# Input weights in 4 KB runs, identity and vectors on ScalarE's queue, and x1's shift as an addition

## The reference

```python
u = layernorm(x) @ W_in.T + b_in
s_t = tanh(u_t + s_(t-1) * gamma + beta)        # 1024 steps, one after another
x1 = x + layernorm(states @ W_out.T + b_out)
gate = silu((layernorm(x1) @ q(gate_w)) * gate_scale)
up = (layernorm(x1) @ q(up_w)) * up_scale
out = x1 + layernorm(((gate * up) @ q(down_w)) * down_scale)
```

## Time and profile before

| | |
|---|---|
| Median of 3 runs | 557.77 us (557.42 to 558.75) |
| The profiled execution | 557.68 us |
| its span | 555.9 us |
| PE busy | 537.8 us, 97% |
| DVE busy | 446.1 us, 80% |
| ACT busy | 374.8 us, 67% |
| POOL busy | 247.6 us, 45% |
| DMA | 39.92 MB in 25333 packets |

### The profile page before, as it was taken

The page is one execution under the profiler, slowest core; times in us unless marked ns, Lnnn a source line. Parts: engine busy times, 40 slices in busy tenths (PEclk is TensorE's granted clock), DMA queues, the critical chain, the costliest instruction groups (busy, mean ns, idle before and its releaser), DMA issues.

```text
span 555.9 us, 11947 instructions
## 1 busy us (share of the span) xinstructions
PE 537.8 (97%) x2958; PEld 456.6 (82%) x2958; DVE 446.1 (80%) x2608; ACT 374.8 (67%) x2317; POOL 247.6 (45%) x372
## 2 busy tenths in 40 slices
PE   7999989899998999999999999999999999999995
PEld 5875768788788788889889888988888888899994
DVE  3699999888797998888897888778987988885414
ACT  2677695865678677877788667876677767662332
POOL 1213454857449343653248243562351343635532
PEclk9999999999999999999999999999999999999998
DMA  8886789973104200130003000300002000100011
GB/s 262 254 265 191 152 200 227 182 171 57 48 15 150 59 2 2 38 97 2 1 2 113 21 1 2 106 11 2 1 2 77 1 2 1 64 16 1 1 39 38
DMA packets 25333, 39.92 MB, mean 72 GB/s; under 512 B 3760, under 2 KB 8496, under 8 KB 25264
## 3 DMA queue, kind: packets, MB, share of 16 engines
q1 hardware_dynamic: 19904, 30.24, 17.0%
q0 software_dynamic: 4608, 8.39, 8.8%
q10 hardware_dynamic: 752, 0.54, 0.3%
HBM read 26.57 MB, written 4.20 MB: 55 GB/s over the span
## 4 chain that ended last, share of the span: by engine, by line
PE 64%; DVE 6%; ACT 2%; issue 0%; POOLq 0%; DVEq 0%; POOL 0%; ACTq 0%
PE gate_up L1130 26%; PE wide L1086 15%; PE wide L1160 13%; PE wide L1055 10%; DVE recur L1230 2%; ACT pairs L1555 1%; DVE recur_second L1230 1%; PE wide L1106 1%; ACT pairs L1540 1%; DVE fused L1363 1%; DVE z L1376 0%; DVE stats_z L1244 0%; DVE x_lo L1345 0%; ACT gated L1590 0%; DVE x_res L1303 0%
## 5 line engine op out<-in xcount | busy, mean ns | idle before, releaser
L1555 ACT ACTIVATE pairs<-recur 128x8 f32<-128x8 f32 x768 | 137.3, 179 | 89.8 <-DVE recur L1230 89.8
L1230 DVE TENSOR_TENSOR_SCAN recur<-recur,pairs 128x16 f32<-128x16 f32 x768 | 150.9, 196 | 49.5 <-ACT pairs L1555 46.8
L1555 ACT ACTIVATE pairs<-recur_second 128x8 f32<-128x8 f32 x768 | 136.7, 178 | 0.0
L1230 DVE TENSOR_TENSOR_SCAN recur_second<-recur_second,pairs 128x16 f32<-128x16 f32 x768 | 133.0, 173 | 0.0
L1753 POOL TENSOR_TENSOR fused_lo<-fused,fused_hi 128x256 fp32r<-128x256 f32 x95 | 70.4, 742 | 128.7 <-ACT fused_hi L1608 128.4
L1086 PE MATMUL wide<-w_out_sb,pairs 128*128 128x512 f32 (+1 forms) x272 | 112.1, 562 | 0.9 <-ACT pairs L1562 0.5
L1055 PE MATMUL wide<-x_norm_t,w_in_sb 128*128 128x256 f32 x448 | 101.9, 380 | 0.9 <-DVE y L1280 0.9
L1086 PEld LDWEIGHTS wide<-w_out_sb,pairs 128*128 128x128 f32 x272 | 75.5, 298 | 26.5 <-ACT pairs L1564 0.8
L1055 PEld LDWEIGHTS wide<-x_norm_t,w_in_sb 128*128 128x128 f32 x448 | 83.7, 190 | 13.1 <-DVE y L1280 1.2
L1160 PE MATMUL wide<-down_q,fused_hi 128*128 128x512 f32 x192 | 82.6, 430 | 0.3 <-POOL fused_lo L1753 0.3
L1590 ACT ACTIVATE gated<-gate_up,gate_scale_cols 128x128 f32<-128x128 f32 (+1 forms) x169 | 63.4, 378 | 26.2 <-PE gate_up L1130 26.1
(11 more groups left out here) (135 smaller groups left out, 795.5 us busy)
## 6 DMA issues: line engine op xcount, KB each, us to landing
x_res<-x SPq DMA_DIRECT2D x16, 256.0 KB, 3.3
x_in<-x SPq DMA_DIRECT2D x14, 256.0 KB, 4.3
out<-z SPq DMA_DIRECT2D x14, 256.0 KB, 2.5
x_norm_t<-x_t SPq DMA_DIRECT2D x5, 512.0 KB, 3.5
raw_own<-rounders POOLq DMA_DIRECT2D x9, 256.0 KB, 5.0
w_in_sb<-w_in_t SPq DMA_DIRECT2D x4, 512.0 KB, 7.5
w_out_sb<-w_out_t SPq DMA_DIRECT2D x8, 256.0 KB, 4.6
raw_own<-down_w SPq DMA_DIRECT2D x8, 256.0 KB, 4.8
```

The source lines that it names most:

```text
L1230: eng.tensor_tensor_scan(preact_of[b].rearrange("p c k -> p (c k)"), factors_of[b].rearrange("p c k -> p (c k)"), pairs[:, t % RING, colum ...
L1555: ins = eng.activation(pairs[:, t % RING + 1, columns, 0], preact_of[b][:, :, 1], ACT.Tanh)
```

## The change

Three edits. The weights `W_in` are laid out by the host so that each quarter is one run of 4 KB for each partition, and `w_in_sb` takes the same layout (quarter, k, 256 columns); PE's reads of it follow. The identity's load moves from SP's queue to ACT's, behind ACT's loads of x, and the vectors b_in, beta and gamma come in one load of 24 floats for each partition in place of three loads of 8. On POOL, `row_shift` gets a factor of -1.0 and x1's shift becomes an addition; in the timetable its length goes from 2.8 steps to 1.8.

```diff
+X1_SHIFT_STEPS = 1.8
...
         side("gpsimd", ("x1_shift", n, b), [(v, 0.2) for v in rows("r", "r_norm", n, b)] + [(("y_shift", n, b), 0.0)], k + 20,
-             NORM_STEPS)
+             X1_SHIFT_STEPS)
...
-        w_in_sb = sb("w_in_sb", [P, KD, hidden])
+        w_in_sb = sb("w_in_sb", [P, MS, KD, 2 * P])
...
-                eng.dma_start(ident[:, :], identity).then_inc(s_ident_in, 16)
                 for m in range(MS):
                     yield HEAD + 1 + m
-                    ms = slice(2 * m * P, 2 * (m + 1) * P)
-                    eng.dma_start(w_in_sb[:, :, ms], w_in_t[:, ms].rearrange("(k p) h -> p k h", p=P)
+                    eng.dma_start(w_in_sb[:, m, :, :].rearrange("p k h -> p (k h)"), w_in_parts[m, :, :]
                                   ).then_inc(s_w_in_in[m], 16)
...
                             ins = eng.matmul(first_u_bank(j),
-                                             w_in_sb[:, k, j * P:(j + 1) * P], x_norm_t[:, k, 0:P],
+                                             w_in_sb[:, j // 2, k, j % 2 * P:(j % 2 + 1) * P], x_norm_t[:, k, 0:P],
                                              start=(k == 0), stop=(k == KD - 1))
...
-                eng.wait_ge(s_small_in, 48)
+                eng.wait_ge(s_small_in, 16)
...
                     eng.dma_start(x_in[1:P:batch, g, :], x_blocks[0][1][:, g, :]).then_inc(s_first_x_in[g], 16)
+                eng.dma_start(ident[:, :], identity).then_inc(s_ident_in, 16)
                 yield HEAD + 0.5
-                eng.dma_start(cols[:, 0, :], b_in).then_inc(s_small_in, 16)
-                eng.dma_start(cols[:, 1, :], beta).then_inc(s_small_in, 16)
-                eng.dma_start(cols[:, 2, :], gamma).then_inc(s_small_in, 16)
+                eng.dma_start(cols[:, :, :].rearrange("p v j -> p (v j)"), u_columns).then_inc(s_small_in, 16)
...
-                    eng.tensor_tensor(row_shift[:, b:b + 1], mean_var["y"][:, b, 0:1], rstd["y"][:, b:b + 1],
-                                      ALU.mult).then_inc(s_row_shift, 1)
+                    eng.tensor_scalar(row_shift[:, b:b + 1], mean_var["y"][:, b, 0:1], rstd["y"][:, b:b + 1], -1.0,
+                                      ALU.mult, ALU.mult).then_inc(s_row_shift, 1)
...
                     eng.tensor_scalar(x_res[n % 2][:, b, :], x_res[n % 2][:, b, :], row_shift[:, b:b + 1], 1.0,
-                                      ALU.subtract, ALU.mult).then_inc(s_x1_shifted, 1)
+                                      ALU.add, ALU.mult).then_inc(s_x1_shifted, 1)
```

More of the change, by code:

```diff
@@ L519, with recurrent_sandwich_kernel @@
          "first_u": (26, 28, 30, 32), "first_u_copy": (31, 33, 35, 37)}
-def recurrent_sandwich_kernel(nc, x, x_t, w_in_t, w_out_t, b_in, beta, gamma, b_out, gate_w, up_w, down_w,
+def recurrent_sandwich_kernel(nc, x, x_t, w_in_parts, w_out_t, u_columns, b_out, gate_w, up_w, down_w,
                               gate_scale, up_scale, down_scale, identity, out):
     batch, seq, dim = x.shape
-    hidden = w_in_t.shape[1]
+    hidden = w_out_t.shape[0]
     inner = gate_w.shape[1]
@@ L1027, in project_first_u @@
                             ins = eng.matmul(wide[quad][:, jj * P:(jj + 1) * P],
-                                             w_in_sb[:, k, j * P:(j + 1) * P], x_norm_t[:, k, P:2 * P],
+                                             w_in_sb[:, j // 2, k, j % 2 * P:(j % 2 + 1) * P], x_norm_t[:, k, P:2 * P],
                                              start=(k == 0), stop=(k == KD - 1))
@@ L1055, in project_u @@
                                 ins = eng.matmul(wide[bank][:, jj * TOK:(jj + 1) * TOK],
-                                                 w_in_sb[:, k, j * P:(j + 1) * P], x_norm_t[:, k, :],
+                                                 w_in_sb[:, j // 2, k, j % 2 * P:(j % 2 + 1) * P], x_norm_t[:, k, :],
                                                  start=(k == 0), stop=(k == KD - 1))
@@ L1798 @@
         "x_t": a["L0_attn_x"].transpose(2, 1, 0).reshape(a["L0_attn_x"].shape[2], -1),
-        "w_in_t": a["L0_attn_W_in"].T,
+        "w_in_parts": a["L0_attn_W_in"].T.reshape(-1, P, a["L0_attn_W_in"].shape[0] // (2 * P), 2 * P).transpose(2, 1, 0, 3).reshape(
+            a["L0_attn_W_in"].shape[0] // (2 * P), P, -1),
         "w_out_t": a["L0_attn_W_out"].T,
-        "b_in": columns(a["L0_attn_b_in"]),
-        "beta": columns(a["L0_attn_beta"]),
-        "gamma": columns(a["L0_attn_gamma"]),
+        "u_columns": _np.concatenate([columns(a["L0_attn_" + name]) for name in ("b_in", "beta", "gamma")], axis=1),
         "b_out": a["L0_attn_b_out"].reshape(1, -1),
```

## The result

The changed kernel takes 564.1 us (median of 4 runs, 563.4 to 564.3) where the kernel before took 558.0 us beside it (median of 4, 557.4 to 558.8). The ratio is 1.0108, with a 95% interval of 1.0091 to 1.0125: 1.1% slower and clear of the noise, where no measurable change was forecast. The profiled execution took 563.91 us, 6.23 us more than that of before (557.68 us).

The account below looks back on a forecast made before the run. PE was taken as the bound, with only time before 171 us counting. 557.68 less 0.7 (first loads) less 0.4 (x1's shift), with 0 for the order, gave 556.6 us; range 555.0 to 558.9 us.

Parts of the forecast that it names:

- What bounds the kernel: PE, busy 537.8 of 555.9 us and full from 175 to 450 us; time saved before 171 us counts in full.
- Part 1, the identity's landing: At the start, on ACT's queue: landing 4.2 us after issue, at 6.4 us; PE's first product at 8.0 us, 0.7 gained.
- The sum: Whole kernel: 557.68 less 0.7 at the start and 0.4 from x1's shift, 556.6 us; chance 0.45.
- Rival B: At the start: the identity lands late, at 7.8 us, losing 0.3 to 0.8 us; 557.6 to 558.1 us, chance 0.10.
- `w_in` 0.63 us sooner, 4 KB runs, one vector load: First loads: w_in issued 0.63 us sooner, long runs worth 0.1 us, vectors in one load landing by 8.4 us at no cost.
- the cover named: At the start: 1.5 us between the vectors' landing by 8.4 us and PE finishing the first quarter at about 9.9 us.
- Part 2: x1's shifts on POOL: addition takes 0.77 us instead of 2.00, removing a DVE delay near 98 us; gain 0.4 us.
- Rival D: x1's shifts on POOL: the addition stays at 2.00 us, so clashes with DVE cost; 558.1 to 560 us, chance 0.09.
- Part 3, the order: All engines' order, planned with 1.8 steps instead of 2.8: sign unknown, taken as 0, between -1.8 and +1.8 us.
- The range: For the new order's effect: 1.8 us either way, from holes of 0.4 to 1.8 us that one misplaced job costs.
- rival C: Before 171 us: the new order opens a PE hole, as where ACT copies u first; 1.8 us, 558.4 to 560, chance 0.17.

Follow-up runs that it names:

- b1: The kernel before with only the identity's load moved to ACT's queue behind x, w_in still in 1 KB runs: 558.65 us, ratio 1.0019.
- b2: The kernel before with x1's shift as an addition, planned at the old 2.8 steps: 557.31 us, ratio 0.9981.
- a1: The changed kernel with the identity's load back on SP's queue ahead of w_in: 560.58 us, ratio 1.0047.
- c_runs_act: The kernel before with the identity on ACT's queue behind x and w_in in 4 KB runs: 562.37 us, ratio 1.0074.
- a2: The changed kernel with the old order (x1's shift planned at 2.8 steps): 561.25 us, ratio 1.0056.
- a3: The changed kernel with both the identity back on SP's queue and the old order of 2.8 steps: 558.37 us, ratio 0.9996.
- b4: The kernel before with w_in in 4 KB runs alone: 558.00 us, ratio 0.9996.
- c_ident_first: The changed kernel with the old order and the identity issued first on ACT's queue, ahead of x: 556.69 us, ratio 0.9979.
- c_price_13: The kernel before with the addition, x1's shift planned at 1.3 steps: 559.35 us, ratio 1.0036.

## Why the prediction was wrong

**What bounds the kernel** held in the main. The shift made before 177 us was carried to the end, and PE was full from 200 to 450 us; its last hole had moved from 170.91 to 177.13 us, into the first of the eleven stretches. What it left out is that PE's work behind that hole isn't fixed: where the clock falls there, up to 1.6 us more are lost (last section).

**Part 1, the identity's landing: the first step that failed.** I took 4.2 us from the row of `b_in`; it took 6.7. The row was of the wrong kind twice: a 4 KB load instead of 64 KB, and read while `w_in` stood behind the identity in runs of 1 KB. The changed runs were in the same diff, and b1 against the four profiles with 4 KB (5.2 against 5.7 to 6.7 us) speaks for it that they hold up the other queue's loads. The sum had 0.7 us gained here; 2.8 us were lost. Rival B named the place, even the rule, but I put its landing at 5.6 us and so priced it at a loss of 0.3 to 0.8 us where 2.8 came. About half of what B lacks is landing time (first product at 10.39 us, where B had 9.0 to 9.5); the rest, 1.13 us, is a term that neither the sum nor the rival had: TensorE's clock after the wait.

**`w_in` 0.63 us sooner, 4 KB runs, one vector load.** The issue moved as said (1.98 us). The gain couldn't show, since the identity came later still. The vectors as one load landed 7.3 us after issue, not 5.6; DVE's sum waited 0.73 us, under the cover named.

**Part 2** was right: 0.69 us a shift in place of 2.00 (I had said 0.77), the operation of 0.86 us gone, and 0.4 us gained in the changed kernel and in b2. Rival D falls. The Trainium skill's GPSIMD Engine Reference, section 3.1, gives 768 ns for 512 elements as its best case; the measured 689 ns lie below it, and the measurement decides.

**Part 3, the order, taken as 0: the other step that failed.** It cost 4.0 us, the larger miss of the two; 0.8 of it goes with the clock again: in a1 the clock stayed up and this loss is missing. The range had 1.8 us either way, one hole of PE's; rival C had the sign and the mechanism (a new hole before 171 us, 2.46 us at 149.41) with a chance of 0.17 and a price of half. Its cause is not ACT's order, as I thought: 1.85 us are DVE operations that came to lie under POOL's, 0.91 us is DVE's wait for a weight, 0.45 us are two small shifts that I haven't followed, and the clock is the rest. Nothing in the trace of before told the new places; but the clash of the earlier trace rows cost 0.43 us because the shift had been nearly over, and an operation of DVE that meets one of POOL near its start can wait out nearly all of it (1.27 us at 124.34 already in before, 1.82 in the changed kernel). No single loss was above the 1.8 us of the range; the range failed because it allowed for one misplaced job, and six losses came.

**The sum.** Expected 557.68 - 0.7 - 0.4 + 0 = 556.6. Found 557.68 + 2.79 - 0.14 - 0.44 + 4.02 = 563.91. Both failed terms had been called unknown or low in price and both went the same way; the upper end of 558.9 us had been made from one of them at a time.

## What to carry to other kernels

A small load on which the first work depends goes ahead of every large one, on any queue: issued first it landed in 1.8 us, issued after `w_in` in 5.2 to 6.7. When a diff both lengthens the runs of a large load and moves a small one beside it, price the small one by a row under the new load or keep the far end open. And where a planner writes the order, a cost that is closer to the truth is no better by itself (for an operation of 0.69 us, 1.8 and 1.3 steps both wrote an order that was worse than that of 2.8, by about 2 us in the medians beside before): change the operation, keep the order that was measured, and read the new order's trace for two-port operations that now meet.

## What the runs showed of the hardware

**TensorE's clock after a hole.** In the changed kernel it fell to 0.50 behind an idle time of 2.54 us; behind 2.46 us at 149.41 likewise (0.55 from 150 to 153 us). Whether it falls isn't fixed by the length of the hole: behind 2.49 us at 146.71 us in the kernel with the identity on SP it stayed at 1.00, and there the 0.8 us lost at step 274 are missing. At the start it fell behind 1.40 us in c_runs_act (0.50 from 11 to 13 us) and stayed at 1.00 behind 1.59 us in b1. And the hole near 170 us, of 1.75 to 1.82 us in the kernels with the old order, goes with the two groups of executions. The first row is of the changed kernel with old order and identity first, the second of that with block 0 at 2.8, in the same stretch:

```profile
171.00:174.00 3.00, 3.00 (x18) 3.00 (x18) 1.95 (x16) 2.23 (x17) 3.00 (x4) 0.58 0.90 225
```

```profile
171.00:174.00 3.00, 3.00 (x26) 2.91 (x25) 1.95 (x16) 2.34 (x17) 3.00 (x4) 1.00 0.79 243
```

Both had idled before, 1.76 and 1.75 us. Where the clock falls, PE does 18 products instead of 26, and the scans lose 1.5 to 1.6 us from step 300 to step 450, in each of the seven profiles with such a fall (a2, a3, b1, b4, c_runs_act, c_ident_first, c_price_13). That is most of the 1.9 us between the groups. The mean clock of an execution tells the group: 0.996 to 0.998 in the 14 lower times of before, 0.993 to 0.995 in the 11 higher. Filling that hole was not tried in any of these kernels, so that the fall makes the groups is read from profiles and clocks and not tested.

**Some operations of DVE wait for a whole one of POOL.** `x_res` takes 0.46 us alone and 1.82 us under a POOL operation of 1.84 that had begun 0.30 us before. The Trainium skill (SBUF — State Buffer, Who interferes with whom) calls the port pair that the two engines share an exclusive lock, and says that an operation of DVE with two inputs in SBUF contends with one of POOL that reads SBUF. The trace agrees to 0.3 us: the blocked one ends at 140.33, POOL's at 140.05. It isn't so for every operation: a BATCH_NORM_STATS2 at 131.20 us took its usual 0.27 us under POOL's of 1.87 that had begun at 130.36.

**A load's landing goes with its place and with the other queue's pieces** (identity on ACT's queue: 5.2 us with runs of 1 KB beside it, one profile; 5.7 to 6.7 with 4 KB, four profiles; 1.8 when it leaves first, one profile; on SP's queue ahead of `w_in` 2.9 to 4.0, once 5.2).
